# Router scores of a decoder layer: weights' high and low parts as one stationary operand, folded by one matmul

## The reference, cut to what matters

```
q = einsum('bsd,rd->bsr', x, Wq_w)            # 16 router dimensions
scores = einsum('bsr,er->bse', q, keys)       # 64 experts
top_vals, top_idx = top_k(scores, 16)
top_w = softmax(top_vals)                      # scattered over 64 experts: gate
z = einsum('bsd,nd->bsn', x, A_w)              # 512 = 64 experts x rank 8
out = einsum('bsn,on->bso', z * gate, B_w) * 2
```

## Time and profile before

| | |
|---|---|
| median of 3 runs | 3342.89 us (3342.78 to 3346.8) |
| profiled execution | 3344.4 us |
| its span, first to last instruction | 3342.6 us |
| mean granted TensorE clock | 0.964 |
| PE busy | 3121.7 us, 93% of the span |
| PEld / DVE / ACT / POOL busy | 78% / 56% / 39% / 26% |

### The profile page before, as it was taken

One profiled execution on the slowest core, in us unless ns is written; L12 is line 12 of the kernel. 1 busy time (PEld: TensorE's weight loads), 2 busy tenths in 40 slices (PEclk: granted clock), 3 DMA queues, 4 the chain that ended last, 5 costly groups with the idle time before them and its releaser, 6 DMA issues. The chain is left out here.

```text
span 3342.6 us, 67169 instructions
## 1 busy us (share of the span) xinstructions
PE 3121.7 (93%) x26008; PEld 2597.5 (78%) x26008; DVE 1863.0 (56%) x4727; ACT 1305.2 (39%) x3580; POOL 871.0 (26%) x751
## 2 busy tenths in 40 slices
PE   5899999997799999999999999999999589999997
PEld 3777787775588888888878888888887478888886
DVE  6688888886443324443253333333334378888885
ACT  2677777775211111111111111111111367777773
POOL 2222222211234322343235332343323000000000
PEclk8899999998699999999999999999999699999998
DMA  7776776771323122221144111221211775556551
GB/s 234 186 196 176 184 171 179 179 178 42 102 83 89 64 56 65 83 83 53 55 158 145 51 63 58 76 83 51 64 57 70 185 191 147 147 147 151 150 146 34
DMA packets 226622, 386.87 MB, mean 116 GB/s; under 512 B 55953, under 2 KB 177393, under 8 KB 225794
## 3 DMA queue, kind: packets, MB, share of 16 engines
q1 hardware_dynamic: 224978, 373.59, 40.8%
q10 hardware_dynamic: 1328, 8.99, 0.8%
HBM read 291.59 MB, written 90.91 MB: 114 GB/s over the span
## 5 line engine op out<-in xcount | busy, mean ns | idle before, releaser
L731 ACT ACTIVATE L_probs<-L_masked,L_least 112x375 f32<-112x375 f32 x1024 | 624.7, 612 | 111.5 <-DVE L_least L864 107.9
L864 DVE CUSTOM_DVE_ANT_0 L_masked<-L_scores,L_nmask 112x375 f32<-112x375 f32 x1024 | 550.6, 543 | 184.8 <-PE L_scores L471 144.5
L1420 PE MATMUL sa_banks<-sa_x_hi,sa_w_hi 128*128 128x480 f32 (+2 forms) x1536 | 558.5, 364 | 2.4 <-DVE sa_x_lo L1681 2.4
L476 PEld LDWEIGHTS L_turned<-L_ident,L_probs 112*125 112x125 f32 x3072 | 460.0, 191 | 129.0 <-issue 44.7
L476 PE MATMUL L_turned<-L_ident,L_probs 112*125 112x112 f32 x3072 | 536.1, 284 | 18.0 <-DVE L_probsT L858 14.3
L1420 PE MATMUL sa_banks<-sa_x_hi,sa_w_lo 128*128 128x480 f32 (+2 forms) x1536 | 549.1, 357 | 0.0
L1420 PE MATMUL sa_banks<-sa_x_lo,sa_w_hi 128*128 128x480 f32 (+2 forms) x1536 | 548.4, 357 | 0.0
L471 PE MATMUL L_scores<-L_krep,L_qrep 128*112 128x376 f32 x1024 | 421.4, 412 | 19.4 <-DMA L_qrep<-query_parts 13.7
L726 ACT COPY L_probsT<-L_turned 125x336 f32<-125x336 f32 x672 | 293.3, 436 | 263.4 <-PE L_turned L476 262.2
L1722 DVE TENSOR_TENSOR sa_acc<-sa_acc,sa_banks 128x512 f32<-128x512 f32 x224 | 153.9, 687 | 418.0 <-PE sa_banks L1479 418.0
L1479 PE MATMUL sa_banks<-sa_p_hi,sa_o_hi 128*128 128x512 f32 x896 | 365.6, 408 | 0.0
(11 more groups left out here) (291 smaller groups left out, 5203.6 us busy)
## 6 DMA issues: line engine op xcount, KB each, us to landing
L_qrep<-query_parts SPq DMA_DIRECT2D x256, 224.0 KB, 6.3
sa_raw<-in_wqkvU_dram SPq DMA_DIRECT2D x96, 512.0 KB, 3.7
L_krep<-ctx_parts SPq DMA_DIRECT2D x256, 188.0 KB, 4.3
sa_raw<-in_wprojU_dram SPq DMA_DIRECT2D x64, 512.0 KB, 3.7
query_parts<-L_qT_hi SPq DMA_DIRECT2D x64, 224.0 KB, 8.7
query_parts<-L_qT_lo SPq DMA_DIRECT2D x64, 224.0 KB, 9.6
L_xcur<-x SPq DMA_DIRECT2D x32, 448.0 KB, 5.4
L_val<-in_ctx_dram SPq DMA_DIRECT2D x64, 187.5 KB
```

The lines of the kernel that those rows point to most:

```text
L476: mm = pe.transpose(turned[0:TC, m % 2, S * j:S * j + S], probs[0:S, m % 4, TC * j:TC * j + TC], ident[0:S, 0:S])
L731: nc.scalar.activation(probs[0:S, e % 4, :], masked[0:S, e % 4, :], ACT.Exp, bias=least[0:S, e:e + 1], scale=-1.0, accum_out=rsum[0:S, e:e ...
L864: v.tensor_tensor_reduce(out=masked[0:S, n % 4, :], in0=scores[0:S, (NH * t + n) % 3, 0:T], in1=nmask[0:S, :], scale=1.0, scalar=HUGE, op0 ...
L1420: mm = pe.matmul(feat[u % 2][i][:, 0:t.stop - t.start], a[:, u % 2, k, :], b[:, k, t], start=(n == 0), stop=(n == 3 * KT - 1))
```

## The change

The router weights' high and low parts are put side by side in one tile `r_both` (128 x 8 x 2 x 64), and they, not the row's features, become the stationary operand. For each of the 8 slices of features one matmul with 128 stationary columns multiplies both parts by `tT_hi` (112 moving columns), and one with 64 stationary columns multiplies the high part by `tT_lo`. The result stands turned, experts x rows: high part's scores in partitions 0 to 63, low part's in 64 to 127. ACT copies it to `scT` at step 21; at step 22 a float32 matmul with `scT` as stationary operand and `fold` (two identity matrices of 64, one above the other) as moving one adds the halves and turns them back. All 16 matmuls stand at step 20, behind a wait for both halves of `tT_lo`; the four `NARROW` matmuls of step 19 go to later steps.

```diff
-        ROUTER, NARROW = ((20, 12), (22, 12)), ((19, 4), (20, 1), (22, 1), (23, 5), (24, 3), (26, 4), (27, 3), (28, 3))
+        NARROW = ((22, 3), (23, 4), (24, 3), (26, 5), (27, 5), (28, 4))
...
-                    if n in (19, 20):
-                        pe.wait_ge(lo2_ok, w.next(lo2_ok))
-                    i, j = dealt(ROUTER, n)
-                    if i < j:
-                        mm = products(wide[0:S, 1, 0:NE], (tT_hi, tT_lo), (r_hi, r_lo), slice(0, NE), KT, i, j)
-                        if j == 3 * KT:
-                            mm.then_inc(rscore_ok, 1)
+                    if n == 20:
+                        pe.wait_ge(lo2_ok, w.next(lo2_ok, 2))
+                    if n == 20:
+                        def high(k):
+                            return pe.matmul(wide[:, 1, 0:S], r_both[:, k, :, :].rearrange("p a e -> p (a e)"), tT_hi[:, k, :],
+                                             start=(k == 0), stop=(k == KT - 1))
+
+                        high(0)
+                        for k in range(KT):
+                            pe.matmul(wide[0:NE, 1, 0:S], r_both[:, k, 0, :], tT_lo[:, k, :], start=False, stop=False)
+                        for k in range(1, KT):
+                            mm = high(k)
+                        mm.then_inc(rscoreT_ok, 1)
+                    if n == 22:
+                        pe.wait_ge(scT_ok, w.next(scT_ok))
+                        pe.matmul(wide[0:S, 1, 256:256 + NE], scT[:, :], fold[:, :], start=True, stop=True).then_inc(rscore_ok, 1)
...
+                if on(-1) and n == 21:
+                    act.wait_ge(rscoreT_ok, w.next(rscoreT_ok))
+                    nc.scalar.copy(scT[:, :], wide[:, 1, 0:S]).then_inc(scT_ok, 1)
...
-                    v.tensor_copy(sc[0:S, :], wide[0:S, 1, 0:NE]).then_inc(sc_read, 1)
+                    v.tensor_copy(sc[0:S, :], wide[0:S, 1, 256:256 + NE]).then_inc(sc_read, 1)
...
+                v.tensor_tensor(fold[:], ident[:, 0:NE], ident[:, NE:P], ALU.add)
```

More of the change, by code:

```diff
@@ L163, in token_stage @@
             out_read, sc_read = s("out_read"), s("sc_read")
+            rscoreT_ok, scT_ok = s("rscoreT_ok"), s("scT_ok")
             res_ok, rscore_ok, top_ok, z_hi_ok, z_lo_ok = (s("res_ok"), s("rscore_ok"), s("top_ok"), s("z_hi_ok"), s("z_lo_ok"))
             a_hi, a_lo = sb("a_hi", [P, KT, BN], F32R), sb("a_lo", [P, KT, BN], F32R)
-            r_hi, r_lo = sb("r_hi", [P, KT, NE], F32R), sb("r_lo", [P, KT, NE], F32R)
+            r_both = sb("r_both", [P, KT, 2, NE], F32R)
+            scT, fold = sb("scT", [P, S]), sb("fold", [P, NE])
             b_hi, b_lo = sb("b_hi", [P, 4, D], F32R), sb("b_lo", [P, 4, D], F32R)
@@ L816, in high_router @@
                 act.wait_ge(r_ok, 1)
-                nc.scalar.copy(r_hi[:], turned[:, 0, :].rearrange("p (k e) -> p k e", k=KT)).then_inc(r_hi_ok, 1)
+                nc.scalar.copy(r_both[:, :, 0, :], turned[:, 0, :].rearrange("p (k e) -> p k e", k=KT)).then_inc(r_hi_ok, 1)
             def load_expert(i):
@@ L1071, in low_router @@
                 dve.wait_ge(r_hi_ok, 1)
-                v.tensor_tensor(r_lo[:], turned[:, 0, :].rearrange("p (k e) -> p k e", k=KT), r_hi[:].bitcast(F32), ALU.subtract)
+                v.tensor_tensor(r_both[:, :, 1, :], turned[:, 0, :].rearrange("p (k e) -> p k e", k=KT),
+                                r_both[:, :, 0, :].bitcast(F32), ALU.subtract)
+                v.tensor_tensor(fold[:], ident[:, 0:NE], ident[:, NE:P], ALU.add)
                 v.tensor_scalar(nmask[0:S, :], nmask[0:S, :], -1.0, None, ALU.mult)
```

## The result

Before 3343.96 us (median of 20 runs, 3340.24 to 3347.45), after 3384.94 us (20 runs, 3343.03 to 3389.47): 1.0101 times the time, 95% interval 1.008 to 1.0121. That ratio is of the means, which hold all 20 runs; the medians alone give 1.0123. The forecast was 3380 us, in 3344 to 3398. The profiled execution took 3384.71 us (span 3382.9), with a mean granted clock of 0.953 against 0.964.

What follows compares the result with a forecast made beforehand. PE was taken as the bound, except once an item, when DVE's burst delays tT_lo. 3344.4 + 1.5 (order) + 36 (clock) = 3381.9 us profiled; as that lies 1.5 above the median, 3380 us was predicted, range 3344 to 3398.

Steps and rivals of the forecast that it cites:

- The bound: Last stage, steady part: PE bounds, but once an item DVE does, PE waiting 1.12 us for tT_lo behind DVE's backlog.
- DVE's burst doesn't depend on PE in this stretch: DVE's work ahead of tT_lo, busy 9.84 of 10.2 us, sets its time; the second half comes no sooner.
- The router's price: PE, per item: 2.36 us of old matmuls replaced by 1.56 us of new ones with fold, 0.80 us less.
- The fold: PE, behind the router: a float32 matmul recorded as two, 2 x 0.098 = 0.20 us an item.
- ACT's copy: ACT, behind step 21's exponential: 128 x 112 copy, 0.25 us, hidden; PE's wait for it taken as none.
- Rival D: Fold waits for ACT's copy, half a microsecond late each item, clock not falling: +8 us, 3352; 4%.
- The wait: PE at step 20, waiting for both tT_lo halves: grows from 1.12 to about 2.05 us, absorbing the 0.80 us saved.
- the +0.1 that I took: Net cost of the new order per item at full clock, from 0 to +0.15 us; +1.5 us over 15 items.
- The clock: Behind most step 20 waits PE's clock falls, costing 1.7 to 5.1 us, taken as 2.4; 36 us over 15 items.
- B: The wait grows but the clock stays at 1.00: only +1.5 us, 3343 to 3346, no change; 20%.
- C: The wait doesn't grow because tT_lo is ready when PE comes; whole saving counts, 12.9 us less, 3330; 8%.

Runs made afterwards that it cites:

- the kernel with NARROW at step 19: Changed kernel with the four NARROW matmuls put back to step 19 and separate waits for the tT_lo halves at steps 19 and 20: 3328.16 us, ratio 0.9956.
- both edits on DVE: Changed kernel, NARROW back at step 19, half of DVE's output statistics moved to step 20, tT_lo written before masked scores: 3313.91 us; same DVE edits on kernel before: 3335.66.
- the kernel with the filled wait: Changed kernel plus four unused 512-column matmuls in PE's wait at step 20: 3344.35 us, ratio 1.0004.

## Why the prediction was right

**The bound.** That PE waits for `tT_lo` only was right. That the time of `tT_lo` is set by DVE's backlog was right for the change, because nothing ahead of it moved. As a statement of cause it was half right: "DVE's burst doesn't depend on PE in this stretch" holds only while the burst is that long. Take the backlog away, and PE's own scores of step 18 are as good as late (0.16 us gained of 0.9).

**The router's price.** Eleven spacings of before said 0.098, and rows of layer 0 said 0.111 and 0.058: measured 0.111 and 0.059. The saving of 0.80 us was 0.92 (the kernel with NARROW at step 19) to 0.97 (with both edits on DVE). The fold is a pair of entries an item. With NARROW at step 19 the fold and the 512-column matmul behind it take 2946.39 - 2945.96 = 0.43 us, of which the matmul usually takes 0.23: 0.20 for the fold, as reckoned.

```profile
2945.96 0.32 PE L689 MATMUL L_wide<-L_fold,L_scT 128*112 128x64 f32 x2
...
2946.39 0.39 PE L464 MATMUL L_spare<-L_a_hi,L_tT_lo 128*112 128x512 f32 x1
```

Where do the 0.12 us on top come from? Before, then with NARROW at step 19, the scores of step 31 and of the step behind it, with the load for the turn of `z` times the gate between them before:

```profile
2965.37 0.41 PE L471 MATMUL L_scores<-L_krep,L_qrep 128*112 128x376 f32 x1
2965.69 0.39 PEld L653 LDWEIGHTS L_spare<-L_ident,L_zg 112*128 112x128 f32 x4 [0.16 <-DVE L_zg L987]
2966.39 0.41 PE L471 MATMUL L_scores<-L_krep,L_qrep 128*112 128x376 f32 x1
...
2957.61 0.41 PE L473 MATMUL L_scores<-L_krep,L_qrep 128*112 128x376 f32 x1
2958.50 0.40 PE L473 MATMUL L_scores<-L_krep,L_qrep 128*112 128x376 f32 x1
```

From the first NARROW matmul behind the wait to the scores of step 31 it is 2965.37 - 2948.20 = 17.17 us before and 2957.61 - 2941.20 = 16.41 here, 0.76 less: the router and the fold save what was reckoned, 0.80. The next step takes 1.02 us before and 0.89 here: before, the load waited 0.16 us for DVE's product, and here it did not. So most of what came on top is this other wait, which the prediction did not have. No faster load for 128 columns showed: 0.111 us against 0.098 for 112 columns. The Trainium skill ("TensorE: Matmul & The Clock Gate", section "Weight-path perf modes — Fast Weight Load (FWL) and DoubleRow") has a fast load on at 128 columns where the type isn't float32. The trace disagrees for float32r, unless that counts as float32; the profile's rows write it as f32.

**ACT's copy.** Reckoned at 0.25 us, measured 240 ns:

```profile
L795 ACT COPY L_scT<-L_wide x16: 240/240/252, 2707.0 to 3352.1; 128x112 f32<-128x112 f32 x16
```

PE waited for it only in the last item, where there are no heads, 0.34 us. Rival D is out.

**The wait.** Reckoned to grow from 1.12 to 2.04 us from start to start. Measured 2.14 less the 0.24 that the scores take: 1.90. The kernel with the filled wait gives the cost of the order at full clock: 40.95 us an item against 40.99, in place of the +0.1 that I took.

**The clock.** That the clock falls behind these waits was right. The size of the term was not: 2.4 us an item, measured (613.79 - 573.90) / 14 = 2.85, and 2.9 against the 40.95 at full clock. By the prediction's own rule, that half of the low time is lost, 2.4 us stand for 4.8 us at the lower level; measured were 95.6 / 15 = 6.4, 13 of 6.8 us and two of 3.4. The 4.8 was a choice between 3.4 and 10.2, two falls at other places, and for the longer one the reading was wrong that it was mostly router matmuls. The 24 of them took (3311.82 - 3309.70) + (3314.49 - 3312.37) = 4.24 of the 10.2 us, and most of the rest were NARROW matmuls. So the argument that the shorter new router shortens the fall had no good ground, and that 3380 came within 5 us of 3385 is in part luck. The changed kernel has 37.5 us in the sum (1.5 for the order and 36 for the clock) against 41 measured, nothing for the order and all of it for the clock.

**The rivals.** B, the clock stays up, got 20%, and 4 of 20 runs took its time, 3343 to 3347 us. That the shares agree is luck: I had taken B for another outcome of the whole case, and it is an outcome of a single run. No run here shows what decides between the two. C, the wait doesn't grow, was excluded by the rows and by the trace after, but its number is what the new router reaches in the right order: 3328 measured, 3330 written down. The Trainium skill ("TensorE: Matmul & The Clock Gate", section "Why this matters for your kernels") warns there only of longer idle gaps, which would have given B. The profiled run disagrees: the clock fell behind gaps of 1.73 us idle.

## What to carry to other kernels

A saving on the busiest engine counts only where that engine isn't waiting: cut the period into the stretch that it bounds and the stretch that another bounds, and ask in which one the saved work lies and which work filled the wait until now. An edit that frees PE and also moves its filling behind a wait can pay twice: here a gap of 1.7 us idle, among transposes and scores, cost 40 us in clock, where 1.2 us idle with 0.47 us of matmuls in the gap cost nothing that could be measured. Where work can't be moved forward, put what the waiting engine needs first on the engine that produces it: swapping two calls brought `tT_lo` 0.5 to 0.6 us sooner.

## What the runs showed of the hardware

- The same gap can be harmless or not: with 1.73 us idle in each item the clock fell behind all 15 waits in the profiled run, and four runs of 20 took the time of a run without a fall. With 1.23 us idle and two 512-column matmuls in the gap, no fall showed in the profiled run, and no run of 11 took the longer time. With 1.12 us idle and nothing in the gap it fell once in 13 items, and once behind a gap of 1.38 us.
- A busy PE doesn't bring the clock back at once: low stretches in the steady part were 3.4 or 6.8 us with 16 router matmuls behind the wait and 6.8 or 10.2 us with 24. Whether the number, the shape or the length of what follows does that is not shown; in the last item of the kernel with NARROW at step 19 a low stretch was 10.2 us with the 16.
- Work that nobody needs can pay: 0.47 us of unused matmuls an item made the changed kernel 41 us faster, against before on the same chip.
